# A transformer pipeline on one core: its loads on two queues, and its loops with hinted back edges

## The reference

```python
y = transformer_layer(1, ctx, ctx, ctx, True,  P(0))     # attention + norm + FFN + norm
x = transformer_layer(1, x,   x,   x,   False, P(1))     # attention + norm
x = transformer_layer(0, x,   x,   y,   True,  P(2))     # attention + norm + FFN + norm
out = layernorm(x + cross_attention(x, ctx, mask, wq, wk, wv, wo, bo))

# inside a layer, per head:
dam = gen_dam(alphas, gumbel) == 0                       # a mask made of one row per head, shifted per query
p   = softmax(where(dam, q @ k.T / sqrt(dk), -1e32))
d   = sqrt(clip((sum(p) - cumsum(p)) * |i - j|, 0))
s   = (q @ k.T / sqrt(dk)) * clip(exp(-softplus(gamma) * d), 1e-5, 1e5)
att = softmax(where(dam, s, -1e32)) @ v
```

## Time and profile before

| what | us |
|---|---|
| three runs: median (lowest to highest) | 3268.62 (3266.42 to 3272.2) |
| the profiled execution, its own time | 3272.65 |
| its span, first to last instruction | 3270.9 |
| busy in the span: PE, DVE, ACT, POOL | 2893.2, 2749.2, 2697.2, 771.9 |

### The profile page before, as it was taken

The page is one execution under the profiler, slowest core; times in us unless marked ns, Lnnn a source line. Parts: engine busy times, 40 slices in busy tenths (PEclk is TensorE's granted clock), DMA queues, the critical chain, the costliest instruction groups (busy, mean ns, idle before and its releaser), DMA issues.

```text
span 3270.9 us, 77341 instructions
## 1 busy us (share of the span) xinstructions
PE 2893.2 (88%) x21912; PEld 2153.1 (66%) x21912; DVE 2749.2 (84%) x5899; ACT 2697.2 (82%) x10212; POOL 771.9 (24%) x1114
## 2 busy tenths in 40 slices
PE   2589999999999999999999999999999999999996
PEld 1367666666667666766666666766776666676664
DVE  2588888899888899888889988889988888988883
ACT  0588888889888889888889988888988888898883
POOL 0122222222222222222222222222222222222221
PEclk9799999999999999999999999999999999999998
DMA  5001111001101001111100110100111110011000
GB/s 159 16 26 32 33 31 31 20 24 33 34 28 34 27 18 29 34 30 31 29 21 25 33 33 28 34 27 15 32 34 30 32 29 21 25 34 33 28 18 10
DMA packets 167564, 101.91 MB, mean 31 GB/s; under 512 B 37312, under 2 KB 166908, under 8 KB 167420
## 3 DMA queue, kind: packets, MB, share of 16 engines
q1 hardware_dynamic: 167420, 100.54, 11.0%
HBM read 56.84 MB, written 10.01 MB: 20 GB/s over the span
## 4 chain that ended last, share of the span: by engine, by line
PE 41%; DVE 33%; ACT 13%; issue 8%; SPq 2%; POOL 1%; DMA 1%; DVEq 0%; ACTq 0%; POOLq 0%
PE gen_ps L666 15%; PE gen_ps L803 7%; DVE X L995 6%; ACT E L849 6%; PE scores_ps L710 4%; DVE E L986 4%; PE gen_ps L756 4%; DVE res L1030 4%; DVE X L1005 4%; ACT X L849 3%; PE gen_ps L720 3%; DVE res L1043 3%; DVE nm L1011 3%; PE gen_ps L674 2%; PE gen_ps L766 2%
## 5 line engine op out<-in xcount | busy, mean ns | idle before, releaser
L849 ACT ACTIVATE X<-X,nm 128x128 f32<-128x128 f32 x1536 | 595.7, 404 | 33.1 <-DVE nm L1011 32.5
L849 ACT ACTIVATE E<-scores_ps,nm 128x128 f32<-128x128 f32 x1536 | 542.1, 392 | 45.2 <-DVE nm L978 45.0
L666 PE MATMUL gen_ps<-f_buf,up_w 128*128 128x256 f32 x2048 | 482.1, 386 | 4.7 <-DVE f_buf L469 0.8
L1120 POOL TENSOR_SCALAR_AFFINE_SELECT X<-X 128x1024 f32<-128x1024 f32 x192 | 209.6, 1092 | 1081.9 <-DVE X L1005 1081.9
L803 PE MATMUL gen_ps<-down_w,hidden 128*128 128x256 f32 x2048 | 453.0, 379 | 1.3 <-ACT hidden L498 1.2
L978 DVE TENSOR_REDUCE nm<-scores_ps 128x8 f32<-128x1024 f32 x320 | 390.3, 1220 | 62.4 <-PE scores_ps L710 61.6
L666 PEld LDWEIGHTS gen_ps<-f_buf,up_w 128*128 128x128 f32 x2048 | 380.0, 191 | 87.4 <-DVE hidden L496 23.9
L986 DVE TENSOR_TENSOR_SCAN E<-chain,E 128x1024 f32<-128x1024 bf16 x192 | 430.0, 2239 | 0.0
L995 DVE SCALAR_TENSOR_TENSOR X<-E,rz,decay 128x128 f32<-128x128 f32 x1536 | 426.5, 348 | 2.2 <-DVE E L986 0.5
L803 PEld LDWEIGHTS gen_ps<-down_w,hidden 128*128 128x128 f32 x2048 | 384.1, 190 | 51.7 <-issue 1.6
L849 ACT ACTIVATE X<-scores_ps,nm 128x128 f32<-128x128 f32 x1024 | 360.8, 402 | 69.0 <-DVE nm L978 57.1
(11 more groups left out here) (143 smaller groups left out, 5229.3 us busy)
## 6 DMA issues: line engine op xcount, KB each, us to landing
k_diag<-k_f SPq DMA_DIRECT2D x768, 32.0 KB, 1.9
xk_diag<-xk_f SPq DMA_DIRECT2D x1024, 8.0 KB, 1.7
ctx_f<-in_ctxT SPq DMA_DIRECT2D x32, 256.0 KB, 2.6
ctx_t<-in_ctx SPq DMA_DIRECT2D x32, 256.0 KB, 2.8
x_t<-in_x SPq DMA_DIRECT2D x32, 256.0 KB, 3.2
x_f<-in_xT SPq DMA_DIRECT2D x32, 256.0 KB, 2.6
cx_f<-in_ctxT SPq DMA_DIRECT2D x32, 256.0 KB, 2.7
out<-out_t SPq DMA_DIRECT2D x32, 256.0 KB, 2.2
```

What stands on the lines that cost most here:

```text
L666: mm = nc.tensor.matmul(ps[:, i * T:(i + 1) * T], w[:, k, c * P:(c + 1) * P], src[:, k, :], start=(k == 0), stop=(k == C - 1))
L849: a = nc.scalar.activation(dst[:, cols], src[:, cols], ACT.Exp, bias=minus_max[:, h:h + 1], accum_out=sums[:, h:h + 1])
```

## The change

Weights and norms move from SP to ACT, in order of need, with a semaphore for each group. SP keeps the setup loads, the parts and the Toeplitz pieces, and loads the first group's four activations ahead of the parts; the step list then leaves these four out in its first turn. The waits for weights move from the head of PE's stream to the steps that read them, in the first turn (`first_pair`). The two rows of the mask's first key are cleared by POOL. The norm sums are made by DVE ahead of its first `norm_sums`. Every loop body is one turn, with a hint for its back edge. The step lists are the same.

```diff
-def run_turns(eng, turn_of, body=1):
-    first = GROUPS - (GROUPS - LATEST - 1) // body * body
-    for it in range(first):
+def run_turns(eng, turn_of):
+    for it in range(LATEST + 1):
         turn_of(Now(it))
-    with eng.Fori(first, GROUPS, body) as it:
-        for i in range(body):
-            turn_of(Now(it + i if i else it))
+    with eng.bass.Fori(LATEST + 1, GROUPS, engines=(eng.engine,), hint_back_edge=True) as it:
+        turn_of(Now(it))
...
+        def first_pair(now, d):
+            return now.static and now.it == d
...
         @block.sync
+            for name in EARLY_LOADS:
+                load(Now(0), 0, 0, name)
             sp.wait_ge(parts_ready, 2)
...
         @block.tensor
-            pe.wait_ge(weights_in, 16 * N_WEIGHTS)
+            pe.wait_ge(o_w_in, 16 * 2)
             pe.wait_ge(v_cols_ready, 1)
...
+            pe.wait_ge(up_w_in, 16 * 2)
...
+            pe.wait_ge(fold_w_in, 16 * 2)
...
-            pe.wait_ge(rows_out, 16 * 3)
-            pe.wait_ge(parts_out, PARTS_OUT)
-            pe.wait_ge(dve_ready, 2)
+            pe.wait_ge(first_w_in, 16 * 4)
+            pe.wait_ge(dve_ready, 1)
...
+                elif first_pair(now, d):
+                    wait_apart(pe, dam_ready, 2)
...
         @block.scalar
+            bring(o_w_in, (o_w[0], t["oWT"][0]), (o_w[1], t["oWT"][1]))
+            bring(up_w_in, *((up_w[l], t["w1T"][l]) for l in FFN_LAYERS))
             nc.scalar.preload_act_table_set("natural_log_exp_and_others")
...
-            act.wait_ge(weights_in, 16 * N_WEIGHTS)
-            act.wait_ge(dve_ready, 2)
+            bring(fold_w_in, (k_w[2], t["kWT"][2]), (xq_w, t["wq"]))
...
+            bring(down_w_in, *((down_w[l], t["w2T"][l]) for l in FFN_LAYERS))
+            act.wait_ge(dve_ready, 1)
...
-            run_turns(act, turn_of, 4)
+            run_turns(act, turn_of)
...
             def norm_sums(now, g, d, l, which):
+                if norms_open:
+                    norms_open.clear()
+                    dve.wait_ge(norms_in, 16 * 16)
+                    link(nc.vector.tensor_tensor(norm_b[:, 0:2, :], norm_b[:, 0:2, :], x2_tok[:, :, :], ALU.add))
+                    link(nc.vector.tensor_tensor(norm_b[:, 2, :], norm_b[:, 2, :], y_tok[:, 0, :], ALU.add))
+                    link(nc.vector.tensor_tensor(norm_b[:, 4, :], norm_b[:, 4, :], y_tok[:, 1, :], ALU.add))
...
+            pool.wait_ge(toeplitz_in, 16 * L * 2 * C * 2)
+            for i in range(2):
+                heads = dam_bias[2][i * HALF:i * HALF + 1, 0, :].rearrange("p (h s) -> p h s", s=S)
+                nc.gpsimd.memset(heads[:, :, 0:1], 0.0).then_inc(dam_ready, 1)
```

More of the change, by code:

```diff
@@ L35 @@
 BIAS_COLS = 6
+EARLY_LOADS = ("ctx_f", "x_f", "ctx_t", "x_t")
 ROWS = 3
@@ L541, in _ @@
                 for bank in range(2):
-                    for c in range(C):
-                        h = l * H + c * 4 + bank * 2
-                        for half in range(2):
+                    for half in range(2):
+                        for c in range(C):
+                            h = l * H + c * 4 + bank * 2
                             src = bass.AP(dam_rows_dram.tensor, h * P * 2 * S + S + half * HALF * (2 * S - 1),
@@ L581, in diag_blocks @@
                                      xk_f[rows_j, u[2], b * S:(b + 1) * S]).then_inc(xdiag_in[slot], 16)
[L583 to L594, removed]
-                    sp.dma_start(dst[:, :, :], t[src][tok, :].rearrange("(b s) d -> s b d", s=S)).then_inc(done, 16)
-                elif name == "pad_mask":
-                    read_out(sp, now, d, ("kx",), back=1, apart=True)
-                    sp.dma_start(pad_mask[:, :], bass.AP(t["pad"].tensor, g * T, [[0, P], [1, T]])).then_inc(done, 16)
-                else:
-                    _, last = max((scores_order.late[step] * len(SLOT) + i, step)
-                                     for i, (_, step) in enumerate(scores_order.events) if not layer_step(step))
-                    wait_apart(sp, scores_done, scores_order.upto(now, d, last, 1))
-                    for first in (0, HALF):
-                        sp.dma_start(pad_bias[first:first + 3, :], pad_parts_dram[:, tok]).then_inc(done, 16)
             def store(now, g, d):
@@ L615, in turn_of @@
                     elif step[0] == "load":
-                        load(now, g, d, step[1])
+                        if not (first_pair(now, d) and step[1] in EARLY_LOADS):
+                            load(now, g, d, step[1])
                     else:
@@ L749, in out_proj @@
             def out_proj(ps, now, d, l):
+                if first_pair(now, d):
+                    if l < 2:
+                        pe.wait_ge(rows_out, 16 * 3)
+                    else:
+                        pe.wait_ge(later_w_in, 16 * 5)
                 in_sbuf(now, d, ("o", l), *[("att", u) for u in SLOT if u[0] == l])
@@ L775, in project @@
                     pe.wait_ge(loaded["cx_f"], 16 * (g + 1))
+                if first_pair(now, d) and step in (("v", 2), ("kx",), ("vx",)):
+                    pe.wait_ge(later_w_in, 16 * 5)
+                    pe.wait_ge(rows_out, 16 * 3)
                 if kind == "k":
@@ L797, in down @@
             def down(ps, now, d, l):
+                if first_pair(now, d):
+                    pe.wait_ge(down_w_in, 16 * 2)
                 for b in range(G):
@@ L972, in _ @@
             dve.wait_ge(pool_ready, 1)
-            dve.wait_ge(dve_ready, 2)
+            dve.wait_ge(dve_ready, 1)
+            norms_open = [True]
             def max1(now, d, u):
```

91 lines of the change are left out of this document (49 added, 42 removed).

## The result

The changed kernel took 3229.72 us (median of four runs, 3226.96 to 3232.13) against 3267.52 us for the kernel before on the same chip (3265.71 to 3272.2): a ratio of 0.9879, 95% interval 0.9867 to 0.9891, 37.8 us less. The forecast was 3229. The total is right, but two of its terms were wrong by 2 and 5 us in opposite directions, so that it came out this close is in part luck.

The account below looks back on a forecast made before the run. The prediction saw an 86 us prologue, one chain through SP's single queue, then 29 turns of 96.70 us. -39.9 + 0.7 = -39.2 us gave 3233.5 for a profiled run, 3229 us as median; range 3214 to 3251.

Parts of the forecast that it names:

- The parts at 11.4 us: Prologue: DVE's dampening parts, for which SP waits, would be ready at about 11.4 us, nearly as before.
- the setup loads are held up by ACT's megabytes: Prologue rival: ACT's 2.6 MB delay SP's small loads by 7 us; 25 us gained, 3244 us; chance 0.07.
- dam_rows issued at 13.8: SP's queue: dam_rows would go out at 13.8 us instead of 25.74, 11.9 us earlier.
- dam_rows takes 19.2 us from issue: Prologue transfer: issued at 13.8, landed at 33.0 us, the middle taken between 25.5 and 40.5.
- First k_diag at 51.4: SP's queue: first k_diag issue at 51.4 us, between 43.9 and 58.9, against 91.27; 39.9 us earlier.
- Nothing else late: Prologue: PE's keys at about 37 us and ACT's issues, ending about 30 to 40, all precede SP's first k_diag.
- ACT still issuing when the keys are there: Prologue sign that the forecast is wrong: ACT is still issuing transfers when PE's keys are ready.
- The norm sums, 0.7: First turn on DVE: moving the norm sums there would cost 0.7 us, once, taken as exposed.
- Hints 0: Loop back edges: hints and one-turn bodies gain or cost 0; ACT's 11.9 us of stalls were hidden.
- Turns stay at 96.7: Loop: the turns would still average 96.7 us, untouched by the change.
- turns settle at another length: Loop rival: PE's clock share shifts, all 29 turns shorter (-22 us, 3207) or longer (+22, 3251); chance 0.05 each.
- The sum: Whole kernel: -39.9 us for the prologue plus 0.7 for the norm sums gives -39.2 us.

Follow-up runs that it names:

- up_w behind the logarithms: The changed kernel with the two up_w loads (2 MB) moved on ACT's queue from ahead of the three logarithms to behind them; 3238.81 us, ratio 0.9909.
- the norm rows held back: The changed kernel with ACT issuing the 16 norm rows and the later and down weights only once dam_rows has landed; 3234.81 us, ratio 0.9896.
- the kernel with the loops alone: The kernel before with only the loop change: one-turn bodies, every back edge hinted, prologue as before; 3265.71 us, ratio 1.0.
- two queues: The changed kernel with row_bias before dam_rows' wait, 10 of 24 Toeplitz loads on ACT's queue, late weights behind ACT's first keys; 3227.05 us, ratio 0.9875.
- layer 0 first: The changed kernel, unhinted, row_bias before dam_rows' wait, layer 0's 8 Toeplitz loads before the first k_diag, late weights behind the first keys; 3230.18 us, ratio 0.9885.
- 25 unread matmuls: The changed kernel with 25 matmuls a turn that nobody reads, put where PE waited; 3190.01 us, ratio 0.9777 to the kernel before.
- the late weights behind the exponentials: The unhinted kernel with layer 0's Toeplitz loads first, its later and down weights moved behind the first turn's second exponentials; 3224.86 us, ratio 0.9863.

## Why the prediction was right in its sum, step by step

- *The parts at 11.4 us*: 14.1. This was the rival "the setup loads are held up by ACT's megabytes", in small. It was priced at 7 us and not taken into the sum; the start moved by 1.8 us (8.59 to 10.39), and from there to the parts it took 3.74 us, as before. The other 0.9 is what the forecast had taken off by letting ACT begin at 8.43 instead of 9.30. The run with up_w behind the logarithms shows the cause: with 2 MB less ahead, 6.34.
- *dam_rows issued at 13.8*: 16.0, the same 2.2 us.
- *dam_rows takes 19.2 us from issue*: 14.1. This is the mis-sized term. The prediction took the middle of its bounds; the near end, running alone (11.7), was closer, and the 12.49 of before closest. With the norm rows held back it measured 13.2, fully contested 23.6 (up_w behind the logarithms). The Trainium skill (DMA: Bandwidth & Descriptors, "Issuing engines are not separate DMA queues") has transfers of two issuers interleave on the same engines. The contested run agrees, at about half the pace; in the changed kernel ACT's queue did not fill the engines (0.90), and the cost was 0.9 us.
- *First k_diag at 51.4*: 48.63, since the two errors, +2.2 and -5.1, cancel in part; that is luck.
- *Nothing else late*: true of PE (keys at 35.4, forecast 37). ACT's issues were to end between 30 and 40: 37.3, and they held the keys back from 35.4 to 37.44. So the prediction's sign of being wrong, ACT still issuing when the keys are there, did appear, but SP's 10 us more covered it. (Between the logarithms and the first `k_f` stand 31 issues, 29 of them large, not 33 and 31; the sum of 10.75 MB holds.)
- *The norm sums, 0.7*: 0.8. They took 1.56 us (98.45 to 100.01), and the first residual came 47.5 us behind the first scores instead of 46.7.
- *Hints 0*: the taken edges cost nothing, right. Leaving the loop had been given 0 to 2.0 us; DVE alone idled 4.1, and from its last back edge to the end it took 2.7 us more than before (89.2 against 86.5).
- *Turns stay at 96.7*: 2706.5/28 = 96.66. The rival "turns settle at another length" named the cause, PE's clock, and later kernels show both its directions, 2699.9 and 2716.3.
- *The sum*: -39.2 forecast, -37.8 by medians. Span to span the gain was 43.1, of which 42.0 outside the loop; the profiled execution of before was 5.1 us above its median here, which is the difference. Some 3 us of it stand in the prologue: the kernel with the loops alone has the prologue of before, and its first k_diag went out at 88.22, not 91.27.

## What to carry to other kernels

Price a transfer beside another queue from two rows, its pace alone and the engines' share at that time: here the time was nearly that alone (14.1 us against 13.2) where the other queue left a share free, and nearly twice it (23.6) where it filled the engines. When a step of a prologue is pulled forward, ask which bulk load it now runs beside: with up_w behind the logarithms, with two queues and with layer 0 first, an earlier issue was paid back by a slower transfer. And where a repeating turn comes in two lengths with equal work on every engine, read the granted clock turn by turn before tuning anything else: 25 unread matmuls were worth 33 us by ratio, beside the 40 of the whole change.

## What the hardware showed that was not expected

- In the changed kernel's loop no wait of PE's matmuls was longer than 2.0 us, in a turn where PE is busy 92% of the time, and yet the clock fell in each of the 28 turns. The Trainium skill (TensorE: Matmul & The Clock Gate, "A second HAM failure mode: psum-queue depth-cycling") describes short idles between groups of matmuls in each iteration that make the clock swing; the turns above agree, with one fall in each; between a turn at a clock of 0.98 and one at 0.96 lie 1.2 us.
- The same 64 one-column folds took 10.71 us in the changed kernel and 13.81 with the late weights behind the exponentials; that is why its keys were late. Rows of PE, after, then there:

```profile
16.60 10.71 PE L614 MATMUL gen_ps<-bias_cols,up_w 128*128 128x1 f32 x64
```

```profile
16.61 13.81 PE L618 MATMUL gen_ps<-bias_cols,up_w 128*128 128x1 f32 x64
```

The profile gives the slower ones a clock of 1.00, but its record of the clock begins at 38.21 us in that trace, and a stretch without a record reads as 1.00 (so do the first stretch of the earlier trace rows and the row with up_w behind the logarithms above). The count of matmuls tells more. The same two windows, after, then there:

```profile
16.60:20.10 3.50, 3.50 (x32) 3.50 (x32) 3.50 (x16) 0.00 (x0) 0.77 (x1) 1.00 1.06 341
20.10:27.30 7.20, 7.20 (x36) 7.20 (x35) 5.71 (x30) 0.00 (x0) 0.00 (x0) 0.50 0.85 238
```

```profile
16.60:20.10 3.50, 3.50 (x18) 3.49 (x17) 3.50 (x16) 0.00 (x0) 0.77 (x1) 1.00 1.07 336
20.10:27.30 7.20, 7.20 (x36) 7.20 (x35) 5.70 (x30) 0.00 (x0) 0.00 (x0) 1.00 0.86 239
```

In the changed kernel the folds start 0.112 us apart until the clock falls, and 0.213 apart at 0.5. In the other kernel they start 0.213 apart from first to last: the pace of the lower level. The changed kernel's record begins at 16.72 us at the higher level, so its folds had that level for their first 3.4 us and the others never. Why an execution starts its folds at one level or the other stays open. In before, the folds lie on the chain: its profiled execution had the slow ones throughout (13.81 us), and the kernel with the loops alone, with the same prologue, the faster form (10.85), and the first k_diag 3 us sooner.
